# Two empty half periods removed from a pipelined attention, and its PSUM banks split three for scores, two for row maxima

## The chip, the core and the metric

The kernel runs on one core of one Trainium2 chip. The time is device microseconds of that core, for one launch that does the whole layer. It keeps five engines in step by semaphores: PE (TensorE, matrix products), ACT (ScalarE), DVE (VectorE), POOL (GpSimd) and SP, which here only issues DMAs. PSUM, where PE writes its products, has eight banks of 512 float32 columns for each of the 128 partitions.

## The reference

A decoder layer with post-layernorm on `x` (8 sequences of 512 tokens, width 256), in float32:

```python
x = _layernorm(x + _L0_attn_ref(x, Wqkv, Wout))            # 16 heads of 16, rotary q and k, softmax
x = _layernorm(x + _L0_xattn_ref(x, ctx, ctx, w_q, ...))   # 16 heads of 16, biases, softmax
x = _layernorm(x + _L0_ffn_ref(x, gate_w, we_gate, ...))   # 8 experts, top 2, plus shared experts
```

Each of the 16 attention instances (self and cross, for 8 sequences) computes `softmax(q k^T / 4) v` for 16 heads over 512 keys. The change touches the two attentions alone.

## The kernel before, in words

**Instances and halves.** An attention instance is (SELF, b) or (CROSS, b) for sequence b. The program walks through *periods* k, each with a FIRST half, whose instance is (SELF, k), and a SECOND half, whose instance is (CROSS, k-1). A half has 16 *steps*; a step does one block of 128 keys for four heads. The halves that exist run in this order: self 0, self 1, cross 0, self 2, cross 1, ..., self 7, cross 6, cross 7. Between self 0 and self 1 lies the SECOND half of period 0, for which there is no instance (it would be cross -1), and between cross 6 and cross 7 the FIRST half of period 8 (it would be self 8). These are the two empty half periods. They run all their steps, but only with the side tasks of their table and the maxima that run ahead. Periods 2 to 6 are a hardware loop (`Fori`).

**One step on PE** (function `half` of the PE block): for j = 0..3 a score product `ps_sc` (L725, 50 rows x 512 columns, keys on the partitions) and a product `ps_max` (L711, 48 rows x 512 columns, queries on the partitions). Before j = 2 come the head outputs `ps_out` (L742, eight rows of the profile for four heads) of the step before, which need all four exponentials of that step. After j = 1 stands a small transpose of the negated maxima (`nm0`, `nm1`, L697) in one step of four, and after j = 3 the side job of the step, if it has one.

**The two chains beside it.** ACT takes the exponential of each score bank (L477, `prob<-ps_sc`). The maximum that it needs is already inside the score product, as two extra rows of q ("mrows"), because the maxima run 7 steps (`LEAD`) ahead: DVE reduces each `ps_max` bank to one column (L519, `nm<-ps_max`), PE transposes them, ACT and DVE split them into a high and a low part, and SP writes them into row 48 and 49 of `qk`.

**The banks.** Of the eight banks two are for side jobs (`ps_job`), one for head outputs, and five for these products: `NSC, NMX = 2, 3`. Score product n goes to bank n % NSC and waits until the exponential n - NSC is done; maximum product n goes to bank n % NMX and waits until reduction n - NMX is done. PE works its queue strictly in order, so whatever it waits for, all behind it waits too.

**Side tasks.** The tables `TASKS` say at which step which projection, transpose or normalization of a neighbouring sequence is done: `q, k, v, cq, ck, cv` are projections (L629, six products of 512 columns or twelve of 256), `ot` four head transposes (L682), `nt, xt` transposes (L665), `w` the output projection, `ln` the layernorm, `x, c` the split of an input. A side job on PE stands at the end of its step; what ACT and DVE do with its result stands at the *start* of their next step, ahead of that step's exponentials and maxima. On DVE that is for `q, k` the pair L535, L536, for `cq, ck` L503 behind ACT's L388, for `ot` L561, L563, for `nt, xt` L501 or L503 behind ACT's L386 or L388, for `w` L581, L585, L588, for `ln` L597.

**SP.** Projected q and k of an instance are written to HBM (`hbm_self`, `hbm_cross`) and read back in another layout by twelve DMAs for each group of four heads (`stack`), which write `qk`.

Behind the attentions, from about 1150 us, comes the phase of the experts, which the change doesn't touch.

## Time and profile before

| | |
|---|---|
| three runs | 1589.96, 1599.72, 1615.62 us; median 1599.72 |
| the profiled execution | 1609.8 us, its span 1608.1 us, mean granted clock 0.915 |
| busy, of the span | PE 89%, DVE 69%, ACT 56%, weight loads 53%, POOL 27% |
| self 0 starts its scores | 61.1 us |
| self 1 starts its scores | 173.5 us |
| cross 0 starts its scores | 230.8 us |
| cross 6, cross 7 start their scores | 996.5 us, 1094.5 us |

Times of one execution are read from the span's start. In a row of the timeline stand the start, the length, the engine, the line, the operation, output<-input, and in brackets how long the engine had been idle and for whom. Lengths of matrix products are modelled ends and overlap: two products of the row-tiled pair `ps_sc`, `ps_max` run at the same time on different rows of the array. PEclk is the clock that PE was granted: 1.0 is 2.4 GHz, 0.5 is 1.2 GHz.

### The profile page before, as it was taken

The page shows a single profiled execution, that of the slowest core. Times are in us where ns is not written, and L with a number is a line of the kernel's source. Part 1 is how long each engine was busy: PE and PEld are TensorE (multiplying, and loading weights), DVE is VectorE, ACT ScalarE, POOL GpSimd, SP SyncE. Part 2 cuts the span into 40 slices and gives each one's busy share as a digit, 9 for nine tenths or more (in the row PEclk, how much of TensorE's full clock was granted, in tenths as well). Part 3 has the DMA queues.
Part 4 walks back from the last instruction along what each step waited for, and adds up shares of the span by engine and source line. Part 5 has one row for each costly group of instructions (what it writes and reads, how often), then busy time and mean ns, then how long its engine had stood idle before and what let it go on. Part 6 is the DMA issues. An engine that isn't in the chain of part 4 may idle for free. (4 is left out here: it accounts for less than half of the span.)

```text
span 1608.1 us, 27690 instructions
## 1 busy us (share of the span) xinstructions
PE 1434.6 (89%) x8424; PEld 857.3 (53%) x8424; DVE 1113.8 (69%) x2282; ACT 907.7 (56%) x1702; POOL 439.8 (27%) x411
## 2 busy tenths in 40 slices
PE   2987999999999999999999999979768898999994
PEld 2424434435444444454444443343357788999974
DVE  3725788879788889889879877648146654555566
ACT  3361576756666666666766765725425444656544
POOL 4004022014013104104104201100005443666654
PEclk8676899989999999999999997987669889999997
DMA  3313343333333333234234233031035425677662
GB/s 125 115 57 111 110 127 106 122 116 113 109 115 128 103 119 116 76 136 128 78 135 135 87 116 120 2 112 35 1 113 183 147 103 126 133 151 159 136 183 89
DMA packets 108089, 179.85 MB, mean 112 GB/s; under 512 B 20288, under 2 KB 65984, under 8 KB 103872
## 3 DMA queue, kind: packets, MB, share of 16 engines
q1 hardware_dynamic: 93376, 159.11, 30.9%
q0 software_dynamic: 14592, 19.41, 6.7%
q8 instruction: 42, 0.69, 0.2%
q14 instruction: 79, 0.65, 0.1%
HBM read 98.09 MB, written 79.30 MB: 110 GB/s over the span
## 5 line engine op out<-in xcount | busy, mean ns | idle before, releaser
L477 ACT ACTIVATE prob<-ps_sc 128x512 f32<-128x512 f32 x1024 | 557.6, 597 | 272.4 <-PE ps_sc L725 267.8
L519 DVE TENSOR_REDUCE nm<-ps_max 128x1 f32<-128x512 f32 x1024 | 640.7, 681 | 94.3 <-PE ps_max L711 94.3
L711 PE MATMUL ps_max<-qk 48*128 48x512 f32 x1024 | 451.9, 509 | 33.7 <-DVE nm L519 23.0
L725 PE MATMUL ps_sc<-qk 50*128 50x512 f32 x1024 | 415.6, 477 | 41.0 <-ACT prob L477 40.7
L725 PEld LDWEIGHTS ps_sc<-qk 50*128 50x128 f32 x1024 | 170.0, 192 | 370.0 <-ACT prob L477 306.9
L742 PE MATMUL ps_out<-prob,va 128*32 128x512 f32 x2048 | 288.0, 636 | 1.3 <-ACT prob L477 1.2
L711 PEld LDWEIGHTS ps_max<-qk 48*128 48x128 f32 x1024 | 182.6, 198 | 93.1 <-DVE nm L519 73.9
L1475 PE MATMUL ps_gu<-x2f,we 128*128 128x256 f32 (+1 forms) x1344 | 223.8, 321 | 4.5 <-ACT sg L1140 2.4
L1475 PEld LDWEIGHTS ps_gu<-x2f,we 128*128 128x128 f32 x1344 | 190.5, 192 | 22.2 <-DVE h L1366 3.0
L356 POOL TENSOR_TENSOR rstd<-mv,eps 128x2 f32<-128x2 f32 x32 | 6.5, 203 | 595.8 <-DVE mv L588 595.8
L1475 PE MATMUL ps_dn<-we,hf 128*128 128x256 f32 x864 | 122.8, 298 | 10.6 <-DVE totals L1449 10.6
L1475 PEld LDWEIGHTS ps_dn<-we,hf 128*128 128x128 f32 x864 | 116.8, 205 | 12.1 <-DVE hf L1370 11.6
L629 PE MATMUL ps_job<-xf,w 128*128 128x512 f32 x288 | 86.0, 438 | 22.5 <-POOL xf L331 16.7
L629 PE MATMUL ps_job<-w,cf 128*128 128x256 f32 x576 | 86.5, 303 | 5.1 <-DVE cf L503 1.7
L1064 POOL DMA_INDIRECT slots_x<-x2in,scat x64 | 66.1, 1033 | 87.6 <-DVE r L1306 27.7
L629 PEld LDWEIGHTS ps_job<-w,cf 128*128 128x128 f32 x576 | 76.7, 203 | 17.3 <-issue 11.1
L742 PEld LDWEIGHTS ps_out<-prob,va 128*32 128x32 f32 x2048 | 41.1, 110 | 69.9 <-issue 59.4
L629 PEld LDWEIGHTS ps_job<-xf,w 128*128 128x128 f32 x288 | 55.0, 205 | 43.1 <-issue 25.6
L1078 POOL DMA_INDIRECT sums<-ys,dest x40 | 62.2, 1555 | 49.4 <-DVE dest L1407 26.1
L1078 POOL DMA_INDIRECT x<-ys,dest x40 | 62.1, 1553 | 31.2 <-ACT ys L1205 18.9
L340 POOL TENSOR_TENSOR res<-res,trig 128x512 f32<-128x512 f32 x32 | 41.0, 1280 | 107.3 <-DVE res L536 107.3
L1222 ACT ACTIVATE hf<-h 128x512 fp32r<-128x512 f32 x40 | 25.3, 632 | 63.4 <-DVE h L1424 57.0
(145 smaller groups left out, 1472.9 us busy)
## 6 DMA issues: line engine op xcount, KB each, us to landing
qk<-hbm_self SPq DMA_DIRECT2D x384, 64.0 KB, 2.3
qk<-hbm_cross SPq DMA_DIRECT2D x384, 64.0 KB, 2.3
hbm_self<-stage SPq DMA_DIRECT2D x16, 1024.0 KB, 3.9
hbm_cross<-stage SPq DMA_DIRECT2D x16, 1024.0 KB, 4.8
slots_x<-zeros SPq DMA_DIRECT2D x8, 1360.0 KB, 5.9
xs<-slots_x SPq DMA_DIRECT2D x40, 272.0 KB
weraw<-w_moe SPq DMA_DIRECT2D x11, 768.0 KB
x2in<-x SPq DMA_DIRECT2D x16, 512.0 KB, 4.0
```

The source lines that it names most:

```text
L340: nc.gpsimd.tensor_tensor(rot[:, c, :], rot[:, c, :], trig[:, 1, :], ALU.mult) \
L356: nc.gpsimd.tensor_tensor(rstd[:, at, :], mv[:, at, 1:2], eps[:, at, :], ALU.add) \
L477: nc.scalar.activation(prob[:, s % 2, j, :], ps_sc[:, (HG * s + j) % NSC, :], ACT.Exp, scale=HD ** -0.5).then_inc(exp_done[a], 1)
L519: nc.vector.tensor_reduce(nm[:, g % 2, r:r + 1], ps_max[:, n % NMX, :], axis=AX.X, op=ALU.max, negate=True).then_inc(max_done[a], 1)
L629: ins = nc.tensor.matmul(out, l(a), r(b), start=(n == 0 and k == 0), stop=(n == len(pairs) - 1 and k == len(parts) - 1))
L711: nc.tensor.matmul(ps_max[:, n % NMX, :], qk[rows, 0, pair, P * c:P * c + P], qk[rows, 1, pair, :], start=True, stop=True).then_inc(smax_d ...
L725: nc.tensor.matmul(ps_sc[:, n % NSC, :], qk[rows, 1, h // 2, P * c:P * c + P], qk[rows, 0, h // 2, :], start=True, stop=True).then_inc(st_ ...
L742: ins = nc.tensor.matmul(ps_out[32 * j:32 * j + 32, :], va[:, a, c, HG * g + j, :], prob[:, s % 2, j, :], start=(c == 0), stop=(c == TT - ...
L1064: nc.gpsimd.indirect_dma_start(rows_x, bass.IndirectOffsetOnAxis(ap=scat[:, q, c, t:t + 1], axis=0), xin[:, q, t, :], None, bounds_check=P ...
L1078: nc.gpsimd.indirect_dma_start(x2 if j // NCH else sums, bass.IndirectOffsetOnAxis(ap=dest[:, c, t:t + 1], axis=0), ys[:, c, t, :], None, ...
L1222: nc.scalar.activation(hf[:, p, HI, :, 0:CH], h[:, p, :].rearrange("p (c t) -> p c t", c=IC), ACT.Copy).then_inc(hhi_done, 1)
L1475: ins = nc.tensor.matmul(o, l(a), r(b), start=(n == 0 and k == 0), stop=(n == len(pairs) - 1 and k == len(parts) - 1))
```

## The change

It has two parts. First, the tables are no longer only FIRST and SECOND: a `Half` object carries its own table, instance, neighbours and SP duties. The order becomes lead, own, own0 (self 0), *close* (self 1), *gap*, second(1) (cross 0), the same loop over periods 2 to 6, first(7) (self 7), *close* (cross 6), *gap*, last (cross 7), post. In *close* the side tasks of its own half and of the empty half stand together, up to two jobs a step; it makes its own maxima to step 8, none in steps 9 to 13, and those of the next instance from step 14. The *gap* has 5 steps without scores: 20 maxima of the next instance, `cv`, `nm1` and `cv`. Second, `NSC, NMX = 3, 2`.

```diff
-NSC, NMX = 2, 3
+NSC, NMX = 3, 2
...
+OWN0 = {
+    0: [("qf", 0, 1), ("k", 0, 1)], 1: [("nm0", 1, 0)], 2: [("kf", 0, 1), ("q", 1, 1)], 3: [("k", 1, 1)], 4: [("qf", 1, 1)],
+    5: [("nm0", 2, 0), ("kf", 1, 1)], 9: [("nm0", 3, 0)], 13: [("nm0", 0, 1)],
+}
+GAP, START = 5, 14
...
+    return {
+        0: [("v", 0, b + 1), ("v", 1, b + 1)], 1: [(rows, 1, i), ("ot0", 0, b), ("ot0", 1, b)], 2: [("ot0", 2, b), ("ot0", 3, b)],
+        3: [("nt0", 0, b), ("nt0", 1, b)], 4: [("w0", 0, b)], 5: [(rows, 2, i), ("w0", 1, b), ("c", 0, b)], 6: [("ln0", 0, b)],
+        7: [("xt", 0, b), ("xt", 1, b)], 8: [("ck", 0, b)], 9: [(rows, 3, i), ("cq", 0, b)], 10: [("cq", 1, b)],
+        11: [("ck", 1, b)], 12: [("x", 0, b + 2)], 13: [("x1b", 0, b)] if b + 1 < B else [], 15: [("q", 0, b + 2)],
+    }
...
+    return {1: [("cv", 0, b)], 2: [("nm1", 0, b), ("cv", 1, b)]}
...
+LAST = {
+    1: [("nm1", 1, 1), ("ot1", 0, 0)], 2: [("ot1", 1, 0)], 3: [("ot1", 2, 0)], 4: [("ot1", 3, 0)], 5: [("nm1", 2, 1)],
+    7: [("nt1", 0, 0)], 8: [("nt1", 1, 0)], 9: [("nm1", 3, 1), ("w1", 0, 0)], 10: [("w1", 1, 0)], 12: [("ln1", 0, 0)],
+    13: [("x1b", 0, 1)],
+}
...
+    own.loads = {8: [("x", 1)]}
+    own.table = {**own.table, 11: [("x", 0, 1)], 15: [("q", 0, 1)]}
...
+    own1 = Half("close", close_behind("nm0", 1, 0), [], s1, c0, s0, None, s0, start=START,
+                loads={2: [("c", 0)], 11: [("x", 2), ("xin", 1)]}, cross={10: (0, 0), 13: (0, 1)},
+                stacks={0: (s1, s0, 3), 12: (c0, s1, 0), 13: (c0, s1, 1)}, clear=1)
+    gap = Half("gap", gap_of(0), own1.table[15], None, c0, s1, s0, s1, steps=GAP, start=START - STEPS,
+               stacks={0: (c0, s1, 2)})
...
+    late = Half("close", table, [], c6, c7, s7, (CROSS, B - 3), s7, start=START,
+                loads={2: [("c", B - 1)]}, cross={10: (B - 1, 0), 13: (B - 1, 1)},
+                stacks={0: (c6, s7, 3), 12: (c7, c6, 0), 13: (c7, c6, 1)})
...
-            for k in (-1, 0, 1):
-                half(FIRST, k)
-                half(SECOND, k)
+            for h in before_loop():
+                half(h)
             with eng.Fori(2, B - 1) as k:
-                half(FIRST, k)
-                half(SECOND, k)
-            for k in (B - 1, B, B + 1):
-                half(FIRST, k)
-                half(SECOND, k)
...
+        def maxima_of(h, s):
+
+            if s >= h.start:
+                inst, first = h.nxt, TT * (s - h.start)
+            else:
+                inst, first = h.cur, TT * (s + LEAD)
+            return [(inst, n) for n in range(first, first + TT)] if inst and first < NMAX else []
```

In the loop the order of the instructions is the same on every engine; only the bank and the count in the waits of `ps_sc` and `ps_max` change. Outside it the order moves at these places.

DVE, before: part of the first empty half period, the side tasks of sequence 0 (`nt0`, `w0`, `ln0`, `xt`) with the maxima of self 1, and no exponentials beside them on ACT.

```order
L501 TENSOR_TENSOR cf<-ps_job,cf 128x512 x2
L581 TENSOR_TENSOR res<-ps_job,xin 128x512
L585 BN_STATS st<-res 128x6 x2
L588 BN_AGGR mv<-st 128x2 x2
L519 TENSOR_REDUCE nm<-ps_max 128x1 x4
L581 TENSOR_TENSOR res<-ps_job,xin 128x512
L585 BN_STATS st<-res 128x6 x2
L588 BN_AGGR mv<-st 128x2 x2
L519 TENSOR_REDUCE nm<-ps_max 128x1 x8
L597 TENSOR_SCALAR x<-res,mv,rstd 128x256 x4
```

DVE, now: the same tasks stand in the close half of self 1 (line numbers are those of the changed kernel), each between the four maxima of a step.

```order
L600 TENSOR_TENSOR cf<-ps_job,cf 128x512 x2
L618 TENSOR_REDUCE nm<-ps_max 128x1 x4
L680 TENSOR_TENSOR res<-ps_job,xin 128x512
L684 BN_STATS st<-res 128x6 x2
L687 BN_AGGR mv<-st 128x2 x2
L618 TENSOR_REDUCE nm<-ps_max 128x1 x2
L600 TENSOR_TENSOR mst<-ps_job,mst 16x128
L618 TENSOR_REDUCE nm<-ps_max 128x1 x2
L680 TENSOR_TENSOR res<-ps_job,xin 128x512
L684 BN_STATS st<-res 128x6 x2
L687 BN_AGGR mv<-st 128x2 x2
L618 TENSOR_REDUCE nm<-ps_max 128x1 x4
```

So the tasks that had a half of their own now share their steps with self 1's scores, exponentials and maxima.

PE, now: from the last score product of self 1 to the first of cross 0. This is the whole gap: 20 maximum products, two jobs `cv`, one `nm1`, and at its start the job `q` of sequence 2 and the last head outputs of self 1.

```order
L824 MATMUL ps_sc<-qk 128x512
L810 MATMUL ps_max<-qk 128x512
L727 MATMUL ps_job<-xf,w 128x512 x6
L810 MATMUL ps_max<-qk 128x512 x2
L841 MATMUL ps_out<-prob,va 32x512 x4
L810 MATMUL ps_max<-qk 128x512 x6
L727 MATMUL ps_job<-w,cf 128x256 x12
L810 MATMUL ps_max<-qk 128x512 x2
L796 MATMUL ps_job<-ident,nm 16x128
L810 MATMUL ps_max<-qk 128x512 x2
L727 MATMUL ps_job<-w,cf 128x256 x12
L810 MATMUL ps_max<-qk 128x512 x8
```

Before, PE had in the corresponding place the end of self 0 and then all the jobs of the empty half, of which this is the beginning.

```order
L725 MATMUL ps_sc<-qk 128x512 x2
L629 MATMUL ps_job<-xf,w 128x512 x6
L742 MATMUL ps_out<-prob,va 32x512 x4
L629 MATMUL ps_job<-xf,w 128x512 x6
L682 MATMUL ps_job<-ident,ot 128x128 x8
L629 MATMUL ps_job<-xf,w 128x512 x6
L682 MATMUL ps_job<-ident,ot 128x128 x4
L629 MATMUL ps_job<-xf,w 128x512 x6
```

The projections of sequence 1 seen here moved ahead, into self 0 (`q` of the first half into the step before it), and the transposes behind, into self 1.

## Rows read from the trace of the kernel before

**Rows 1.** Windows, by stage: stretch, us, busy us (count) by engine, PEclk, DMA share, GB/s.
```profile
41.60:61.10 19.50, 18.74 (x41) 10.06 (x42) 15.98 (x28) 0.86 (x2) 0.00 (x0) 0.50 0.46 121
61.10:116.90 55.80, 48.85 (x225) 15.46 (x224) 24.35 (x41) 36.60 (x70) 2.35 (x1) 0.81 0.22 73
116.90:173.50 56.60, 43.32 (x149) 27.24 (x148) 32.26 (x67) 8.35 (x15) 19.27 (x17) 0.62 0.31 93
173.50:230.80 57.30, 52.62 (x303) 21.69 (x302) 43.60 (x72) 40.86 (x78) 5.12 (x5) 0.99 0.41 131
230.80:996.50 765.70, 733.69 (x4317) 352.29 (x4316) 644.96 (x1212) 510.18 (x983) 157.08 (x155) 0.98 0.35 113
996.50:1051.10 54.60, 51.23 (x297) 21.03 (x297) 33.00 (x66) 39.47 (x76) 4.35 (x5) 0.96 0.09 26
1051.10:1094.50 43.40, 32.94 (x130) 20.68 (x129) 27.40 (x56) 6.08 (x10) 4.53 (x8) 0.74 0.37 113
1094.50:1150.00 55.50, 47.97 (x224) 14.96 (x222) 24.45 (x41) 35.50 (x68) 0.00 (x0) 0.81 0.06 18
```

**Rows 2.** Windows, one period of the loop: cross 3 and self 5; columns PE, PEld, DVE, ACT, POOL.
```profile
615.60:677.00 61.40, 59.93 (x365) 29.58 (x364) 54.84 (x106) 42.84 (x83) 19.55 (x17) 1.00 0.30 96
677.00:742.10 65.10, 60.65 (x357) 28.96 (x356) 52.88 (x96) 42.27 (x81) 7.08 (x9) 1.00 0.41 133
```

**Rows 3.** Timeline of PE, one step of self 1 without a side job.
```profile
212.78 0.50 PE L725 MATMUL ps_sc<-qk 50*128 50x512 f32 x1
212.79 0.50 PE L711 MATMUL ps_max<-qk 48*128 48x512 f32 x1
213.97 0.50 PE L725 MATMUL ps_sc<-qk 50*128 50x512 f32 x1 [0.45 <-ACT prob L477]
214.46 0.49 PE L725 MATMUL ps_sc<-qk 50*128 50x512 f32 x1
214.88 1.06 PE L742 MATMUL ps_out<-prob,va 128*32 128x512 f32 x8
215.88 0.50 PE L725 MATMUL ps_sc<-qk 50*128 50x512 f32 x1
```

**Rows 4.** Timeline of DVE and of ACT, the same step.
```profile
213.36 2.48 DVE L519 TENSOR_REDUCE nm<-ps_max 128x1 f32<-128x512 f32 x4 [0.62 <-PE ps_max L711]
...
213.32 2.27 ACT L477 ACTIVATE prob<-ps_sc 128x512 f32<-128x512 f32 x4 [0.83 <-PE ps_sc L725]
```

**Rows 5.** Timeline of PE, then of DVE, a step of cross 3 with a side job.
```profile
617.73 0.50 PE L711 MATMUL ps_max<-qk 48*128 48x512 f32 x1
618.16 1.66 PE L629 MATMUL ps_job<-xf,w 128*128 128x512 f32 x6
...
617.00 2.48 DVE L519 TENSOR_REDUCE nm<-ps_max 128x1 f32<-128x512 f32 x4
619.96 0.69 DVE L535 TENSOR_TENSOR cosq<-ps_job,trig 128x512 f32<-128x512 f32 x1 [0.49 <-PE ps_job L629]
621.22 1.27 DVE L519 TENSOR_REDUCE nm<-ps_max 128x1 f32<-128x512 f32 x2
```

**Rows 6.** Waits of the whole run: engine line <- releaser, us in total, times, longest.
```profile
PE ps_sc L725 <- ACT prob L477: 40.7, 86, 1.3
PE ps_max L711 <- DVE nm L519: 23.0, 43, 1.6
```

**Rows 7.** The page's DMA issues (KB, us to landing), and SP's timeline within one stack.
```profile
qk<-hbm_cross SPq DMA_DIRECT2D x384, 64.0 KB, 2.3
hbm_cross<-stage SPq DMA_DIRECT2D x16, 1024.0 KB, 4.8
...
216.69 5.56 SPq L254 DMA_DIRECT2D qk<-hbm_cross  x10
```

**Rows 8.** Windows, a stretch of the loop at the lower clock, and PE's timeline at it.
```profile
348.50:358.80 10.30, 10.04 (x34) 3.96 (x35) 5.60 (x9) 3.82 (x8) 0.00 (x0) 0.50 0.20 65
...
116.47 2.93 PE L629 MATMUL ps_job<-xf,w 128*128 128x512 f32 x6
```

More of the change, by code:

```diff
@@ L3 @@
 from contextlib import ExitStack
+from dataclasses import dataclass, field
 import numpy as np
@@ L68, in exists, with shifted @@
     return not isinstance(b, int) or 0 <= b < B
+def shifted(table, k):
+    return {s: [(kind, n, k + off) for kind, n, off in table[s] if exists(k + off)] for s in table}
+@dataclass
+class Half:
+    name: str
+    table: dict
+    former: list
+    cur: tuple = None
+    nxt: tuple = None
+    prv: tuple = None
+    older: tuple = None
+    tail: tuple = None
+    steps: int = STEPS
+    start: int = STEPS - LEAD
+    k: object = None
+    loads: dict = field(default_factory=dict)
+    own: dict = field(default_factory=dict)
+    cross: dict = field(default_factory=dict)
+    stacks: dict = field(default_factory=dict)
+    result: dict = field(default_factory=dict)
+    clear: object = None
@@ new lines, in behind_loop @@
+def behind_loop():
+    s7, c6, c7 = (SELF, B - 1), (CROSS, B - 2), (CROSS, B - 1)
+    table = {s: [t for t in row if exists(t[2])] for s, row in close_behind("nm1", B - 2, B - 1).items()}
+    late = Half("close", table, [], c6, c7, s7, (CROSS, B - 3), s7, start=START,
+                loads={2: [("c", B - 1)]}, cross={10: (B - 1, 0), 13: (B - 1, 1)},
+                stacks={0: (c6, s7, 3), 12: (c7, c6, 0), 13: (c7, c6, 1)})
+    gap = Half("gap", gap_of(B - 1), [], None, c7, c6, s7, c6, steps=GAP, start=START - STEPS, stacks={0: (c7, c6, 2)})
+    last = Half("last", shifted(LAST, B - 2), [], c7, None, c6, s7, None, stacks={0: (c7, c6, 3)}, result={14: B - 2})
+    post = Half("post", shifted(TASKS[FIRST], B + 1), [], None, None, c7, c6, c7, result={14: B - 1})
+    return [first(B - 1), late, gap, last, post]
@@ L71, in upto @@
+SPECIAL = [(t, i) for i, t in enumerate(
+    t for h in before_loop()[2:5] + behind_loop()[1:4] for s in sorted(h.table) for t in h.table[s]
+    if t[0] in PER and t[0] not in ("x", "c"))]
+SPECIAL = {t: i % 2 for t, i in SPECIAL}
 def upto(kind, b, n):
@@ L195, in bank, with behind @@
-        def bank(kind, n):
-            return ps_job[:, [t[:2] for t in ORDER].index((kind, n)) % 2, :]
-        def maxima_of(s, cur, nxt):
-            inst, first = (cur, TT * (s + LEAD)) if s + LEAD < STEPS else (nxt, TT * (s + LEAD - STEPS))
-            return [(inst, n) for n in range(first, first + TT)] if inst else []
+                half(first(k))
+                half(second(k))
+            for h in behind_loop():
+                half(h)
+        def behind(h, s):
+            return h.table.get(s - 1, []) if s else h.former
@@ L284, in half @@
-                for s in range(STEPS):
-                    if h == FIRST and s in (1, 6) and exists(k - 1):
-                        m = s // 6
-                        sp.wait_ge(lo_done["cq"], upto("cq", k - 1, m))
-                        sp.wait_ge(lo_done["ck"], upto("ck", k - 1, m))
+                for s in range(h.steps):
+                    if s in h.cross and exists(h.cross[s][0]):
+                        b, m = h.cross[s]
+                        sp.wait_ge(lo_done["cq"], upto("cq", b, m))
+                        sp.wait_ge(lo_done["ck"], upto("ck", b, m))
@@ L331, in split_lo, with half @@
                 nc.gpsimd.tensor_tensor(out, value, high.bitcast(F32), ALU.subtract).then_inc(lo_done[kind], 1)
-            def half(h, k):
-                for s in range(STEPS):
-                    for kind, n, b in tasks(h, s, k):
+            def half(h):
+                for s in range(h.steps):
+                    for kind, n, b in h.table.get(s, []):
                         if kind in ("q", "k"):
@@ L450, in rows_hi, with half @@
                     mrow_wait(cur or prv, 2)
-                split_hi(kind, b, n, mst[:, n % 2, HI, :], bank(kind, n)[0:HG * TT, 0:P])
-            def half(h, k):
-                cur, nxt, prv = instances(h, k)
-                if h == FIRST and isinstance(k, int) and k == 0:
+                split_hi(kind, b, n, mst[:, n % 2, HI, :], bank(kind, n, b)[0:HG * TT, 0:P])
+            def half(h):
+                if h.name == "own0":
                     act.wait_ge(w_ready, 5)
-                older = instances(prv[0], prv[1] + prv[0])[2] if prv else None
-                for s in range(STEPS):
-                    for kind, n, b in former(h, s, k):
+                for s in range(h.steps):
+                    for kind, n, b in behind(h, s):
                         if kind not in ("nm0", "nm1"):
@@ L608, in half @@
                         if j == NM_AT + 1:
-                            for kind, n, b in tasks(h, s, k):
+                            for kind, n, b in h.table.get(s, []):
                                 if kind in ("nm0", "nm1"):
```

245 lines of the change are left out of this document (129 added, 116 removed).

## The prediction

> **What bounds the kernel now.** I read the windows by stage first. From 230.8 to 996.5 us run twelve halves, cross 0 to self 7, in 765.7 us, almost half of the span, at clock 0.98 [rows 1]: whatever the banks do is multiplied there. The empty half periods take 56.6 and 43.4 us; ACT is busy for 8.35 and 6.08 us in them, and the clock is 0.62 and 0.74 [rows 1]. What they hold is worth at most 100 us, and much of it must be done somewhere else.
>
> Then one period of the loop: 61.4 + 65.1 = 126.5 us with DVE busy 54.8 + 52.9 = 107.7, ACT 42.8 + 42.3 = 85.1 [rows 2]. PE reads 120.6, but its lengths are modelled, so I look at what its products wait for. The table of waits gives PE 40.7 us behind exponentials and only 23.0 behind reductions [rows 6]. That speaks for the third score bank, but it counts only time in which no older product was still shown as running. The timelines show more.
>
> In a step without a side job, the products of j = 2 come first in the rows, then those of j = 0 and 1 of the next step. Score product 2 starts at 212.78, its exponential at 213.32, and product 0 of the next step at 213.97, after an idle 0.45; products 1 follow at 214.46, head outputs at 214.88, product 2 again at 215.88 [rows 3, 4]. The step is 3.10 us long, and its chain is 0.54 + 0.65 + 0.49 + 0.42 + 1.00: the score banks set it. In a step with a side job another chain does. DVE's first maximum starts at 617.00; four take 2.48, so with 0.68 for one they start 0.60 apart [rows 5]. The first ends at 617.68, and maximum product 3 starts at 617.73, 0.05 behind it: it waits for n - 3. The job starts 0.43 later (618.16) and is 1.66 long, DVE idles 0.49 for it and starts its task at 619.96, and the next maximum at 621.22 [rows 5]. Product 3 of the next step can start at 621.22 + 0.68 + 0.05 = 621.95: a loop of 4.22 us, through PE's job, DVE's task and the *first* maximum behind it.
>
> **Two maxima banks.** In the step without a job, product 1 of the next step must now wait for the reduction of product 3. Product 2 at 212.79, reductions from 213.36 [rows 3, 4]: the second ends at 213.36 + 0.60 + 0.68 = 214.64, product 1 starts at 214.69, head outputs 0.42 later, product 2 another 1.00 later: 216.11. The step becomes 3.33, 0.23 longer. The third score bank would by itself have let the head outputs start at 213.32 + 0.49 + 0.60 + 0.05 = 214.46 and the step end at 2.68; that gain of 0.42 is lost behind the maximum product, which is in PE's queue ahead of the head outputs.
>
> In the step with a job, product 3 waits for the second maximum and not the first: 0.60 later. The job, DVE's task (it was idle for it) and the next first maximum move by the same 0.60, so each such step pays again: 4.82 for 4.22. Which steps these are, the tables say: all where DVE has a task that depends on the job of the step before: cq, ck twice each, nt1 and w1 twice each in FIRST; q, k, nt0, w0, xt twice each in SECOND: 18 of 32. One of them, the first xt, I take out, since ACT's split of `c` stands in front of its exponentials. 17 x 0.60 = 10.2. The other fifteen: v and cv are followed by no task on DVE and are PE's own length, single steps without a job between others pay little, since their wait is partly paid by the neighbour's; only ln, with four tasks on DVE, costs another 0.6. I add 0.8 for all. That is 11.0 a period, and 6 periods x 11.0 = **66 us** for the twelve halves. Upper bound: all 32 steps by 0.60, 115 us. Lower bound: below zero, because the 40.7 us behind exponentials may go and the maxima be hidden; I put it at -30. I take 66, near the middle, because the step of [rows 5] is what most steps look like.
>
> The trace shows one and the same gap of 0.45 before a score product in the steps without jobs [rows 3]. The Trainium skill, Perfetto Trace Analysis, section Optimization Strategy, says that a gap that repeats on the engine that should be full can mean too few buffers in PSUM. By that rule alone the third score bank would bring back much of the 40.7 us, and the sum would be as in the first rival. It names the right bank for one chain, and doesn't say what the bank taken away was doing.
>
> **The empty halves.** By stage, against [rows 1]:
> - *41.6 to 61.1* (28 maxima at clock 0.5, 19.5 us). With two banks a reduction waits for its product's way: at this clock I take 0.16 more for each, 4.5 us, and the job q of sequence 1 now stands there, up to 2.93 [rows 8], partly hidden: +6 (0 to 8).
> - *Self 0*, 55.8: its last step's projection leaves, three with DVE tasks come in (4.8 each), and the other thirteen steps now all have maxima: 14.5 + 13 x 3.33 + four small transposes of 0.2 = 58.5, +2.7 (0 to 6).
> - *First empty half*, 56.6, goes; the gap of 5 steps comes. 20 maxima at 0.65 to 0.8 are 13 to 16, two jobs cv (1.7 to 2.9) are half hidden: 17 (13 to 22). -39.6.
> - *Self 1*, 57.3, becomes the close half. The nearest rows are the loop's halves, 61.4 and 65.1 [rows 2], which by the sum above become 67 and 70. The close half has a few more side jobs than these, two in a step in places, where DVE does both tasks before it turns to the maxima; but it has no maxima in steps 9 to 13. I take 68; bounds are 61 (a loop half as it was) and 76 (70 and two more job steps' worth of waits). SP's way from the projection to `qk` is 4.8 to HBM, twelve issues at 0.56, 2.3 to land [rows 7], 14 us, against steps 10 to 13, which have two or three jobs and come to about the same: I add 1.5 for a late stack (0 to 5). 69.5, +12.2.
> - *Cross 6*, 54.6, becomes the other close half, without v, x and q, three jobs of 1.66 less [rows 5], some of it covered: 64 + 2 = 66, +11.4.
> - *Second empty half*, 43.4, for a gap of 17: -26.4.
> - *Cross 7*, 55.5: ot1, nt1, w1 join it. Its last steps have no maxima and gain from three score banks (3.1 to 2.7), the others pay: 57, +1.5.
>
> These make 6 + 2.7 - 39.6 + 12.2 + 11.4 - 26.4 + 1.5 = **-32 us**. Bounds of the unknown parts: -45 to -12.
>
> **The clock.** Two stretches of some 10 us in the loop are at 0.5; one is shown [rows 8]. It holds 34 of PE's products in 10.3 us; a step without job has 16, so it takes 4.8 there for 3.1, and one stretch costs about 3 us. The two lie at the end of self 2 and of self 3, where DVE does ln1 and PE waits longest. With 0.6 more waiting in each step I expect it in three more periods: **+9** (0 to 30).
>
> Sum: -32 + 66 + 9 = +43, 1609.8 + 43 = 1653 for the profiled execution, a ratio of 1.027. That execution is 10 us above the median of the three runs; by the ratio on 1599.7 I forecast **1642 us**.
>
> **Rivals.**
> - *The score banks matter, the maxima banks don't.* For it: the waits, 40.7 against 23.0 [rows 6], and ACT's idle 0.83 in each step [rows 4]. Against: product 3 starts just 0.05 behind a reduction [rows 5]. If DVE's queue had room, the halves would keep 765.7 less some 15 to 20, the other stages lose 5 us less, and the clock nothing: 1600 - 32 - 20 = 1548. Chance 0.12.
> - *The two parts cancel.* If in half of the seventeen steps the third score bank or ACT's slack catches the 0.60 (as I assume for one xt), the loop pays 30: 1600 - 32 + 30 + 3 = 1601. For it: several ACT tasks stand in front of exponentials. Chance 0.15.
> - *The clock falls again and again.* PE now stops twice in every step, for DVE. The trace shows 0.98 for the loop [rows 1] and falls only where PE waits longest. If each half had one more stretch at 1.2 GHz of 10 us, 3 to 6 us each in twelve halves with longer jobs (2.93 for 1.66 [rows 5, 8]): 1642 + 50 = 1690 to 1700. Chance 0.12. The Trainium skill, TensorE: Matmul & The Clock Gate, section "A second HAM failure mode: psum-queue depth-cycling", tells of a kernel whose cycling through PSUM banks leaves micro-idles and makes the clock swing. By that rule this case is the likeliest; the trace before, with such waits in every step and the clock at 0.98, bears it out only little.
> - *My forecast*, the chain through the second maximum: 0.61, its own range 1615 to 1675.
>
> **Range and chances.** 1592 to 1695 us: it takes in the whole forecast, most of the cancelling case and most of the clock's. A change of 2% (1568, 1632) is about what this kernel's runs, 1590 to 1616, can tell from none. Faster by more: the first rival, 0.12. Within: the second and the lower fifth of the forecast, 0.29. Slower: 0.59.
>
> **What would show it.** In the loop, a step without job of 3.3 and a job step q or k of 4.8; PE's `ps_max` waits for `nm` up several times, `ps_sc` waits for `prob` nearly gone; period 137 us for 126.5; DVE busy unchanged at 108 in a longer period. The close halves 66 to 70, the gaps 15 to 19. I would be wrong if product 3 starts before the second reduction has ended, which would mean that the banks don't bind as I read them; if the period stays at 127; or if the close halves are far over 70, because a stack or a side task comes late.

## The result and the profile after

The changed kernel took 1675.57 us in the median of four runs (1674.49 to 1684.47), the kernel before, beside it on the same chip, 1598.95 (1589.96 to 1615.62). The ratio is 1.0511, with a 95% interval of 1.0449 to 1.0573: **slower**, by 5% where 2.7% were forecast. (The ratio is that of the means without the execution of 1615.62 us, a slow one, over 1.5% above the fastest of its kernel.) The profiled execution took 1675.1 us (its span 1673.4, mean granted clock 0.901) against 1608.1 for the span before. All stage times below are of these two spans, 65.3 us apart.

The windows by stage, as in [rows 1]: prologue to self 0, self 0, close half of self 1, gap, the twelve halves of the loop, close half of cross 6, gap. A stage begins where its scores start, a gap where the first of its 20 maximum products starts (205.75 and 1137.06). What is called the loop here is the stretch of twelve halves from cross 0 to self 7, of which the ten in the middle are the hardware loop.

```profile
41.60:68.80 27.20, 23.89 (x47) 11.83 (x47) 18.26 (x29) 1.81 (x3) 2.35 (x1) 0.50 0.58 128
68.80:128.60 59.80, 53.20 (x271) 21.50 (x270) 46.80 (x80) 38.57 (x75) 15.34 (x12) 0.97 0.37 114
128.60:205.70 77.10, 70.25 (x349) 33.04 (x349) 42.06 (x78) 45.08 (x83) 9.22 (x10) 0.82 0.38 112
205.70:224.20 18.50, 15.37 (x54) 8.40 (x54) 13.26 (x23) 2.06 (x4) 2.53 (x2) 0.78 0.08 24
224.20:1067.60 843.40, 815.00 (x4307) 387.03 (x4305) 654.61 (x1211) 519.39 (x982) 154.06 (x153) 0.95 0.33 102
...
1067.60:1137.10 69.50, 65.70 (x320) 28.78 (x320) 41.64 (x78) 42.70 (x80) 4.12 (x5) 0.84 0.26 78
1137.10:1156.90 19.80, 16.89 (x54) 8.76 (x54) 12.95 (x21) 2.32 (x5) 0.00 (x0) 0.67 0.21 50
```

The largest number is the loop's: 843.4 us for 765.7 [rows 1], +77.7, with DVE's busy time up by only 10 in it. The empty halves did go (18.5 and 19.8 us stand where 56.6 and 43.4 were), but the halves beside them grew.

One period of the loop, cross 3 and self 5, as in [rows 2], and the first job step of that cross half on PE and DVE, as in [rows 5].

```profile
643.80:710.60 66.80, 65.61 (x365) 31.86 (x364) 55.80 (x106) 43.82 (x83) 19.52 (x17) 1.00 0.29 88
710.60:786.60 76.00, 71.59 (x357) 33.33 (x356) 53.99 (x96) 42.96 (x81) 7.05 (x9) 0.89 0.38 115
```

```profile
645.90 0.50 PE L810 MATMUL ps_max<-qk 48*128 48x512 f32 x1
...
646.50 0.49 PE L810 MATMUL ps_max<-qk 48*128 48x512 f32 x1
646.92 1.66 PE L727 MATMUL ps_job<-xf,w 128*128 128x512 f32 x6
...
651.30 0.50 PE L810 MATMUL ps_max<-qk 48*128 48x512 f32 x1
```

```profile
645.17 2.55 DVE L618 TENSOR_REDUCE nm<-ps_max 128x1 f32<-128x512 f32 x4
```

The first reduction ends at 645.17 + 0.68 = 645.85, and maximum product 2 starts at 645.90; the second ends 0.60 later, at 646.45, product 3 starts at 646.50, and the job behind it at 646.92. Before, product 3 stood 0.05 behind the *first* reduction [rows 5]. From product 3 to product 3 it is 651.30 - 646.50 = 4.80 us; 4.82 was forecast.

That this holds step after step can be read from the starts of the steps. In cross 3, at full clock in both traces, the 16 steps differ from before by 0.59, 0.60, 0.02, 0.59, 0.60, -0.24, 0.01, 0.59, 0.52, 0.60, 0.61, -0.59, 1.20, -0.25, 0.23 and 0.37 us: 5.4 in all, and eight of them by 0.52 to 0.61. The first fourteen steps of self 2 ran at full clock too, before and now, and grew by 5.0:

```profile
291.95:347.44 55.49, 52.83 (x319) 25.90 (x319) 46.28 (x85) 37.90 (x73) 7.08 (x9) 1.00 0.45 145
```

```profile
293.31:353.81 60.50, 57.49 (x320) 27.59 (x319) 47.66 (x87) 38.22 (x73) 7.05 (x9) 1.00 0.44 133
```

A step without a job, on PE and on DVE, as in [rows 3, 4], here from self 0.

```profile
96.26 0.49 PE L824 MATMUL ps_sc<-qk 50*128 50x512 f32 x1
...
98.17 0.49 PE L810 MATMUL ps_max<-qk 48*128 48x512 f32 x1
98.59 1.07 PE L841 MATMUL ps_out<-prob,va 128*32 128x512 f32 x8
99.59 0.50 PE L824 MATMUL ps_sc<-qk 50*128 50x512 f32 x1
```

```profile
96.82 2.57 DVE L618 TENSOR_REDUCE nm<-ps_max 128x1 f32<-128x512 f32 x4 [0.76 <-PE ps_max L810]
```

The step is 99.59 - 96.26 = 3.33 us, as forecast (3.10 before). Product 1 of the next step, at 98.17, stands behind the second reduction (96.82 + 0.60 + 0.68 = 98.10), and the head outputs stand behind it.

The table of waits, as in [rows 6].

```profile
PEld ps_sc L824 <- ACT prob L576: 189.5, 244, 2.5
PEld ps_max L810 <- DVE nm L618: 180.2, 404, 2.1
```

Against those of before:

```profile
PEld ps_sc L725 <- ACT prob L477: 306.9, 444, 2.2
...
PEld ps_max L711 <- DVE nm L519: 73.9, 152, 2.1
```

Waits for a maxima bank went from 73.9 to 180.2 us and from 152 to 404 times; those for a score bank fell from 306.9 to 189.5. In this profile most of a wait for a bank is on the row of the weight load (180.2 us for `ps_max`), and the matmul's own row [rows 6] shows what is left: 23.0 us for `ps_max` are up to 43.5, 40.7 for `ps_sc` down to 5.7. So "`ps_sc` waits nearly gone" holds for the matmul's row alone, and "`ps_max` several times" is 2.4 times on one row and 1.9 on the other.

### The profile page after: what moved, and what is told of

It is laid out like the page before. It is cut to its first block and busy times, and to the rows that moved or that the text cites. A ratio compares the mean times of both kernels' runs of the same rounds, so it can differ in the third digit from the quotient of the medians.

```text
span 1673.4 us, 27725 instructions
## 1 busy us (share of the span) xinstructions
PE 1526.5 (91%) x8424; PEld 901.0 (54%) x8424; DVE 1132.1 (68%) x2282; ACT 917.9 (55%) x1702; POOL 438.7 (26%) x411
## 5 line engine op out<-in xcount | busy, mean ns | idle before, releaser
L618 DVE TENSOR_REDUCE nm<-ps_max 128x1 f32<-128x512 f32 x1024 | 657.5, 684 | 162.4 <-PE ps_max L810 161.8
L576 ACT ACTIVATE prob<-ps_sc 128x512 f32<-128x512 f32 x1024 | 566.5, 597 | 362.9 <-PE ps_sc L824 357.4
L810 PE MATMUL ps_max<-qk 48*128 48x512 f32 x1024 | 473.4, 519 | 60.3 <-DVE nm L618 43.5
L824 PEld LDWEIGHTS ps_sc<-qk 50*128 50x128 f32 x1024 | 179.5, 200 | 291.3 <-ACT prob L576 189.5
L841 PE MATMUL ps_out<-prob,va 128*32 128x512 f32 x2048 | 299.4, 659 | 2.9 <-ACT ot L503 1.7
L810 PEld LDWEIGHTS ps_max<-qk 48*128 48x128 f32 x1024 | 187.2, 201 | 209.6 <-DVE nm L618 180.2
L1573 PE MATMUL ps_dn<-we,hf 128*128 128x256 f32 x864 | 128.5, 307 | 13.3 <-DVE totals L1547 10.5
L1573 PEld LDWEIGHTS ps_dn<-we,hf 128*128 128x128 f32 x864 | 122.2, 214 | 15.1 <-DVE hf L1468 14.5
L727 PE MATMUL ps_job<-xf,w 128*128 128x512 f32 x288 | 88.4, 448 | 20.1 <-POOL xf L433 16.5
L602 DVE SCALAR_TENSOR_TENSOR stage<-ps_job,bcol,stage 128x512 fp32r<-128x512 f32 x32 | 24.0, 751 | 60.2 <-ACT stage L490 60.2
```

Source lines behind the costliest of these rows:

```text
L576: nc.scalar.activation(prob[:, s % 2, j, :], ps_sc[:, (HG * s + j) % NSC, :], ACT.Exp, scale=HD ** -0.5).then_inc(exp_done[a], 1)
L602: ins = nc.vector.scalar_tensor_tensor(out=out, in0=value, scalar=bias, in1=high.bitcast(F32), op0=ALU.add, op1=ALU.subtract)
L618: nc.vector.tensor_reduce(nm[:, g % 2, r:r + 1], ps_max[:, n % NMX, :], axis=AX.X, op=ALU.max, negate=True).then_inc(max_done[a], 1)
L727: ins = nc.tensor.matmul(out, l(a), r(b), start=(n == 0 and k == 0), stop=(n == len(pairs) - 1 and k == len(parts) - 1))
L810: nc.tensor.matmul(ps_max[:, n % NMX, :], qk[rows, 0, pair, P * c:P * c + P], qk[rows, 1, pair, :], start=True, stop=True).then_inc(smax_d ...
L824: nc.tensor.matmul(ps_sc[:, n % NSC, :], qk[rows, 1, h // 2, P * c:P * c + P], qk[rows, 0, h // 2, :], start=True, stop=True).then_inc(st_ ...
```

## The experiments

The theory at the start: product 3 waits for the second reduction, and with it the job, DVE's task and the next reductions; that is the loop's loss. The rivals: it comes with the new halves, from the score banks, or from the clock. The two parts of the change, run apart, are called p1 and p2. Times of stages below are of one profiled execution each, and not all on the same chip; ratios are to the kernel before on the same chip.

**The new halves alone** (p1), with the old banks:

```diff
-NSC, NMX = 3, 2
+NSC, NMX = 2, 3
```

> The new halves with the old banks (two for scores, three for maxima). Theory (the banks cost the time, the halves save some): the twelve halves of the loop stretch are back at 766 us, 61.4 for a cross and 65 for a self half, and the total is the time before less about 30: 1568 (1555 to 1580). Rival (the close halves are where the time goes, through a late stack and a late load of x): the total stays above 1600.

Measured: 1569.26 us (1563.78 to 1570.21), ratio 0.9791 [0.9748, 0.9834]. Its first close half with gap, and the loop:

```profile
118.70:208.60 89.90, 80.92 (x402) 38.09 (x403) 54.02 (x101) 46.70 (x87) 11.74 (x12) 0.86 0.34 99
208.60:969.20 760.60, 727.80 (x4309) 351.24 (x4307) 644.47 (x1211) 509.82 (x982) 154.41 (x153) 0.98 0.37 114
```

The loop is as before (760.6 for 765.7). Taking out the empty halves is by itself a gain of about 2%, and the loop's loss has nothing to do with it.

**The banks alone** (p2), with the old halves:

```diff
-NSC, NMX = 2, 3
+NSC, NMX = 3, 2
```

> The old halves with the new banks (three for scores, two for maxima). Theory: every loop half is as long as in the changed kernel, cross 66.8, twelve halves 843, and the total is 1599 plus 77 plus 5 to 10 for the other halves: 1684 (1675 to 1695), more than the changed kernel. Rival (the halves are to blame): 1600 to 1620.

Measured: 1705.41 us (1695.71 to 1713.16), ratio 1.0645 [1.0587, 1.0703]. The stretch from self 0's scores to self 1's, and the loop:

```profile
66.00:182.90 116.90, 95.30 (x371) 45.47 (x369) 57.96 (x108) 44.33 (x84) 21.64 (x18) 0.73 0.27 80
245.60:1088.30 842.70, 811.81 (x4317) 385.72 (x4316) 655.99 (x1212) 520.01 (x983) 157.00 (x155) 0.96 0.33 103
```

The loop's loss is here: 842.7 (843.4 with both parts), and cross 3 takes 66.8, the same as with both. The total is 21 over what I expected, and that lies outside the loop: 97.1 of span, 77.0 in the loop, 14.8 ahead of it, 5.3 behind. The two parts nearly add up: -39.7 + 97.1 = 57.4 of span, 65.3 with both.

**Neither bank: two and two**, old halves. It tells what each third bank is worth.

```diff
-NSC, NMX = 2, 3
+NSC, NMX = 2, 2
```

> The old halves with two score banks and two maxima banks, one bank of PSUM unused. Theory (the chain through the second maximum sets almost every step, so that a third score bank buys nothing while maxima have two): cross halves of 67 to 68 us, product 3 still 0.60 behind the end of the first reduction, total within 10 us above the kernel with three and two: 1685 to 1695. Rival (the third score bank does pay in the steps without a job and where ACT is late, and hides part of the loss): 0.3 to 0.4 us in each of some 15 steps a period and more, 1705 to 1725.

Measured: 1737.41 us (1730.93 to 1745.77), ratio 1.0851 [1.0793, 1.0909]. Self 0 with the empty half, the loop, cross 3, and everything from cross 7 on:

```profile
65.30:191.50 126.20, 103.42 (x371) 47.99 (x369) 57.79 (x108) 45.34 (x84) 21.62 (x18) 0.64 0.25 75
254.20:1101.20 847.00, 810.64 (x4315) 388.62 (x4314) 657.03 (x1212) 521.35 (x983) 157.03 (x155) 0.95 0.33 102
680.30:747.40 67.10, 65.55 (x366) 32.19 (x365) 55.81 (x106) 43.90 (x83) 19.53 (x17) 1.00 0.28 86
1209.00:1739.00 530.00, 461.86 (x2944) 393.04 (x2942) 277.79 (x726) 252.85 (x459) 227.87 (x197) 0.84 0.45 116
```

In the loop the third score bank buys 847.0 - 842.7 = 4.3 us, 0.3 of a cross half; the third maxima bank, against the kernel before, buys 847.0 - 765.7 = 81.3 us, 67.1 - 61.4 = 5.7 of cross 3. So it is as the theory says there, and the rival of the score banks falls. The total came out over 40 us above my figure, beyond the rival's too (1705 to 1725), and most of that lies where the clock is lower: the first stretch has 0.64 for p2's 0.73 and is 9.3 longer, the last 0.84 for 0.89 and is 530.0 for 514.3. What moves the clock there I did not isolate.

**Head outputs one place earlier**, in the changed kernel: if PE's wait for a maxima bank could stand behind the head outputs, they would hide it.

```diff
-PV_AT = 2
+PV_AT = 1
```

> The changed kernel with the head outputs one place earlier in PE's order, before the products of j = 1 and not of j = 2. Theory: in a step without a side job the head outputs no longer stand behind the maximum product that waits for the last reduction, so these steps go from 3.33 to about 3.15 us; the steps with a job keep their 4.8, since product 3 still waits for the second maximum; total 5 to 12 us less than the changed kernel, 1664 to 1671. Rival (the order on PE is what makes DVE's waits, in all steps): 30 us or more less, below 1645.

Measured: 1737.84 us (1724.50 to 1769.03), ratio 1.0823 [1.0754, 1.0892], 62 more than the changed kernel (50 by the two ratios) where I expected less. PE in self 0, then PE and DVE at the start of cross 3:

```profile
98.70 0.50 PE L810 MATMUL ps_max<-qk 48*128 48x512 f32 x1
99.13 1.06 PE L841 MATMUL ps_out<-prob,va 128*32 128x512 f32 x8
```

```profile
666.27 0.50 PE L810 MATMUL ps_max<-qk 48*128 48x512 f32 x1
...
667.59 0.50 PE L810 MATMUL ps_max<-qk 48*128 48x512 f32 x1 [0.15 <-DVE nm L618]
```

```profile
666.84 1.97 DVE L618 TENSOR_REDUCE nm<-ps_max 128x1 f32<-128x512 f32 x3 [0.19 <-PE ps_max L810]
```

The steps without a job stayed at 3.33 (96.79 to 100.12) and didn't fall to 3.15: the head outputs at 99.13 now stand behind product 0, at 98.70, and that one waits for a second reduction too (97.36 + 0.60 + 0.68 = 98.64). In the step with a job, maximum product 1 now comes behind the head outputs, at 666.27. The second reduction starts late for it (666.84), ends at 667.52, and product 3, which waits for it, starts at 667.59, 2.97 behind product 0 (664.62) where the changed kernel has 646.50 - 643.81 = 2.69. I had counted what the move takes from the score chain and forgotten that the maximum product feeds the very reduction that binds. In this step a late *second* reduction is paid in full, 0.28. It is a small part of the loss: cross 3 takes 70.5 us for 66.8, and it grows most in its steps 2, 5, 6 and 11, by 0.5 to 1.1 each, whose chain was not read.

**The loads of x earlier**, on p1 (new halves, old banks). In the changed kernel's first close half, steps 13 and 14 take 6.95 and 7.73 us. SP, then ACT and PE, there:

```profile
176.59 0.63 SPq L399 DMA_DIRECT2D slots_x<-zeros  x1
...
181.00 1.32 SPq L365 DMA_DIRECT2D raw<-xT  x1
...
184.37 5.54 SPq L352 DMA_DIRECT2D qk<-hbm_cross  x12
```

```profile
188.21 1.06 ACT L488 ACTIVATE xf<-raw 128x1024 fp32r<-128x1024 f32 x1 [3.22 <-DMA raw<-xT]
...
193.98 0.80 PE L810 MATMUL ps_max<-qk 48*128 48x512 f32 x2 [2.90 <-DMA qk<-hbm_cross]
```

The load of `raw` is issued at 181.00, behind the clearing of the experts' buffers, and ACT stands 3.22 us for it, with its exponentials behind. The load of `xin` and then the stack of `qk` (184.37) follow, and PE's maximum products of step 14 stand 2.90 us for the stack.

```diff
-                loads={2: [("c", 0)], 11: [("x", 2), ("xin", 1)]}, ...
+                loads={2: [("c", 0)], 8: [("x", 2), ("xin", 1)]}, ...
```

> The new halves with the old banks, and in the close half of self 1 the loads of x and xin at step 8 of SP's order instead of 11, so that they no longer stand between the write of cross 0's projections and the reading back of its first stack. Theory (these loads and the stack behind them are what made the first close half longer than forecast): ACT no longer waits 3 us for raw, the stack comes 3 us earlier, the first close half and gap go from 89.9 to about 84, the total from 1569 to 1563 to 1565. Rival (the clock and DVE's tasks make the close half long, not SP): no change, 1567 to 1571.

Measured: 1536.70 us against 1577.03 for the kernel before on that chip, ratio 0.9748 [0.9709, 0.9786], the lowest ratio of the runs that compute the whole. The first close half with its gap, self 7, and the second close half with its gap:

```profile
120.50:204.30 83.80, 78.47 (x404) 37.72 (x404) 53.97 (x101) 46.48 (x87) 11.74 (x12) 0.91 0.35 107
907.70:969.50 61.80, 58.20 (x353) 27.09 (x352) 51.24 (x96) 41.61 (x80) 4.55 (x8) 1.00 0.42 131
969.50:1044.00 74.50, 69.33 (x374) 31.93 (x374) 52.57 (x98) 44.23 (x84) 4.13 (x5) 0.97 0.29 83
```

83.8 for p1's 89.9, 6.1 less, as expected, but only half of it is the wait. Step 13 falls from 6.80 to 3.59, which is the 3 us of the theory. Step 8 gives another 2.2 (6.54 to 4.32): it ran at 1.2 GHz in p1 and at 2.4 here, and nothing in the edit is shown to do that. Step 14 still waits for the stack. The total's difference to p1 is within both intervals.

The second close half, with its gap, shows what the clock alone can do. The edit doesn't touch it and its instructions are those of p1, which took 82.2 us for it (969.2 to 1051.4) at clock 0.83; here, on another chip, it is 74.5 at 0.97. Twelve of its sixteen steps are as long to 0.02 us, and nearly all of the 7.7 lies in steps 7 and 8 and in the last one with the gap, where the clocks differ.

**The clearing later too, and a gap of six steps**, on the kernel just seen:

```diff
-GAP, START = 5, 14
+GAP, START = 6, 15
-    return {1: [("cv", 0, b)], 2: [("nm1", 0, b), ("cv", 1, b)]}
+    return {1: [("cv", 0, b)], 3: [("nm1", 0, b), ("cv", 1, b)]}
...
-                    if s == 10 and h.clear is not None:
+                    if s == (15 if h.name == "close" else 10) and h.clear is not None:
```

> As x_load_early, and the clearing DMAs of self 1 at step 15 instead of 10, and the maxima of the next instance begin at step 15 with a gap of 6 steps instead of 14 and 5 (its small transpose one gap step later). Theory (the late stack still holds PE's maximum product in step 14): the wait for qk is gone in both close halves, and since the sixth gap step costs 2.5 to 3 us the total is within 3 us of x_load_early. Rival (the stack costs more than that in both places, since PE stands with everything behind it): 5 to 10 us less than x_load_early.

Measured: 1550.45 us, ratio 0.9841 [0.9799, 0.9883], 14 us more than the run above, where the theory had at most 3 more and the rival less. The first close half with its gap takes 86.4 us, where the five-step gap has 83.8; the second pair takes 78.4 for 74.5. Step 14 no longer waits (4.01 for 6.56 in the first), but the gap grows by more than that. Part of this is the clock again (0.95 for 0.97 in the second pair), and the two profiled executions are equal, 1541.3 and 1540.7 of span, so that the 14 us between the medians can't be placed. By the medians five steps stay.

**PE filled**, banks 2 and 2: two unused products in each step were to keep PE busy, so that the clock stays up and the waits alone remain.

```diff
-NSC, NMX = 2, 3
+NSC, NMX = 2, 2
...
+        ps_fill = ctx.enter_context(nc.psum_tensor("ps_fill", [P, T], F32))
...
+                        if cur and ahead and j % 2:
+                            nc.tensor.matmul(ps_fill[:, :], w[:, HI, 0, 0:P], w[:, HI, 0, 0:T], start=True, stop=True)
```

> The old halves with two and two banks, and in each step with scores and maxima two more products of 128 rows by 512 columns into the unused bank, ahead of the maximum products of j = 1 and j = 3; their result is used by nothing. Theory (PE's longer waits cost a second time through its clock, most of all in self 0, cross 7 and the self halves): the added products stand where PE waits for DVE anyway, the granted clock of the loop goes from 0.93 to near 1, self halves from 76 to 71 or 72, total 1695 to 1715 against 1737. Rival (the clock is not what the wait costs, and added work only lengthens the steps that have no wait): 1745 to 1765.

Measured: 2020.85 us (1996.01 to 2050.97), ratio 1.2768 [1.2678, 1.2858], clock 0.845 in the profiled execution, the longest of the four. The lengthening hides what the run was to show. PE in a cross half, then the whole of self 1:

```profile
891.16 0.50 PE L726 MATMUL ps_sc<-qk 50*128 50x512 f32 x1
891.16 0.50 PE L712 MATMUL ps_max<-qk 48*128 48x512 f32 x1
891.50 0.40 PE L726 MATMUL ps_sc<-qk 50*128 50x512 f32 x1
891.83 0.49 PE L763 MATMUL ps_fill<-w 128*128 128x512 f32 x1
892.25 0.50 PE L712 MATMUL ps_max<-qk 48*128 48x512 f32 x1
```

```profile
213.70:337.30 123.60, 123.15 (x335) 48.01 (x334) 46.98 (x72) 42.15 (x78) 5.09 (x5) 0.50 0.19 60
```

The pair at 891.16 runs side by side; the next two are split by the filler, which takes 0.42, and PE has no gap left in the rows. What the waits cost without the clock can't be read from it. But one thing on the clock can: in self 1 PE was busy for 123.15 of 123.60 us and was granted 1.2 GHz all the time (0.97 in the same half with banks 2 and 2 and no filler). The ends of its products are modelled, but DVE waited 64.8 us for it there: the low clock stood with hardly any idle time of PE.

**The loads of x earlier in the changed kernel**, the same edit with banks 3 and 2:

> The changed kernel, with the loads of x and xin in the close half periods issued at step 8 and not at step 11. Theory (the close halves lost time because the loads of x stood behind the projection's clearing in SP's queue, so that the next stack came late too): step 13 of the first close half falls from 6.95 to about 4, the first close half with its gap from 95.6 to 89 or 90, the whole 5 to 7 us less than the changed kernel, about 1669, a ratio to the kernel before of 1.047. Rival (the stack itself bounds these steps, the load is hidden behind it): close half and gap stay at 95 to 96 and the time at 1675.

Measured: 1666.75 us (1657.05 to 1683.84), ratio 1.0403 [1.0337, 1.0468]. The first close half with its gap takes 90.1 us. Self 7:

```profile
993.20:1060.20 67.00, 63.33 (x351) 29.57 (x350) 52.13 (x96) 42.28 (x80) 4.54 (x8) 1.00 0.39 120
```

90.1 for 95.6, as expected: step 13 gives 3.3 of it (6.95 to 3.62); step 14 is as long as before, 7.75, and waits for the stack; the rest is in step 7 and in the last step with the gap, at other clocks. The total is 9 below the changed kernel, the intervals overlap. This self 7 ran wholly at full clock, as did the one with the old banks above, so 67.0 - 61.8 = 5.2 us is what the banks cost this self half without the clock.

**Short reductions with banks 2 and 3, then 3 and 2**, old halves, both with reductions over 256 columns in place of 512, so that the maxima are over half of the keys:

```diff
-                nc.vector.tensor_reduce(nm[:, g % 2, r:r + 1], ps_max[:, n % NMX, :], axis=AX.X, op=ALU.max,
+                nc.vector.tensor_reduce(nm[:, g % 2, r:r + 1], ps_max[:, n % NMX, 0:T // 2], axis=AX.X, op=ALU.max,
```

> The kernel before (two score banks, three maxima banks), with each maximum reduction over 256 of the 512 columns of its product: the maxima are then over half of the keys, which is the part of the computation that it changes. Theory (a reduction's spacing, 0.60 us for 512 columns, is what the second maxima bank costs): here the spacing is about 0.33; the twelve halves of the loop come out 5 to 25 us below 765.7, since only part of the steps are bound by a reduction. It is the base for the next run. Rival (a fixed latency per bank): no statement on this run alone.

> The same short reductions with three score banks and two maxima banks, the old order of the halves. Theory: product 3 waits for the second reduction, which now ends only 0.33 behind the first: each of 17 steps of a period pays 0.3 or less in place of 0.60, so the twelve halves are 20 to 35 us longer than with banks 2 and 3, not 77, and a cross half 2 to 3 us longer, not 5.4. Rival (what the missing bank costs is a fixed latency between engines, or the score banks' doing, and not the reduction): the twelve halves again 70 to 80 us longer, a cross half 5.4.

Measured: 1555.62 us, ratio 0.9710 [0.9635, 0.9786], and 1583.16, ratio 0.9878 [0.9796, 0.9960]. The loop and cross 3 with 2 and 3:

```profile
221.10:948.40 727.30, 703.04 (x4317) 340.63 (x4316) 458.56 (x1212) 507.73 (x983) 157.23 (x155) 1.00 0.40 119
586.10:646.20 60.10, 58.58 (x365) 28.52 (x364) 39.37 (x106) 42.69 (x83) 19.52 (x17) 1.00 0.34 98
```

With 3 and 2, and then its step 4, DVE and PE:

```profile
227.90:980.50 752.60, 734.26 (x4317) 366.75 (x4316) 462.41 (x1212) 511.69 (x983) 157.13 (x155) 0.98 0.38 115
608.50:669.00 60.50, 60.10 (x365) 30.35 (x364) 39.37 (x106) 42.72 (x83) 19.51 (x17) 0.99 0.32 94
```

```profile
626.38 0.74 DVE L519 TENSOR_REDUCE nm<-ps_max 128x1 f32<-128x256 f32 x2
...
626.85 0.82 PE L711 MATMUL ps_max<-qk 48*128 48x512 f32 x2
```

The wait is still there, with the shorter spacing. The first reduction ends at 626.38 + 0.42 = 626.80 and product 2 starts at 626.85; the second ends at 627.12 and product 3 starts some 0.05 behind it. Step 4 takes 3.23 us (624.96 to 628.19) for 2.90 with banks 2 and 3 (601.99 to 604.89), 0.33 more; with the long reductions it took 3.77 for 3.17, 0.60 more. So the price of the missing bank follows the spacing of the reductions, 0.33 for 0.60, and is no fixed latency.

In the sum that isn't plain. In cross 3 the steps that grow do so by 2.5 us together, which is what I gave the whole half (2 to 3), but others shrink by 2.1 (0.60 in step 11, 0.78 in step 13), and the half is 0.4 longer. That these shrink by the third score bank fits the shorter step 11 in the long-reduction kernels with three of them (2.25 for 2.85 with two) but wasn't run apart here. The loop is 25.3 us longer, within the expected 20 to 35 for a reason that I hadn't given: 2 us of it are in the six cross halves, self 7 has 1.4 at full clock, and much of the rest is the clock of the self halves. At 1.2 GHz are some 37 us of this loop and 3 with banks 2 and 3.

The base run missed its bounds: 38 us below 765.7, not 5 to 25. Cross 3 is 1.3 shorter and self 5 3.7 (65.1 to 61.4), more than I had said, and its loop has clock 1.00 for 0.98.

## Why the prediction was right, and where its sizes were off

Taken in the order of its steps, in spans (before to after):

| step | forecast | measured |
|---|---|---|
| prologue maxima | +6 | +7.7 |
| self 0 | +2.7 | +4.0 |
| first empty half to gap | -39.6 | -38.1 |
| self 1 to close half | +12.2 | +19.8 |
| twelve halves, chain and clock | +66, +9 | +77.7 |
| cross 6 to close half | +11.4 | +14.9 |
| second empty half to gap | -26.4 | -23.6 |
| cross 7 and what follows | +1.5 | +2.9 |
| sum | +43 | +65.3 |

**The chain through the second reduction** is right in place and size. The places: 3.33 and 4.80 per step for a forecast of 3.33 and 4.82, product 3 at 0.05 behind the second reduction. The size: cross 3 pays 66.8 - 61.4 = 5.4 and self 7 5.2 at full clock, 10.6 a period for a forecast of 11.0. Self 7 is a lighter half than those of the hardware loop (61.8 for 65 at full clock); of these none ran through at full clock with the new banks, but the first fourteen steps of self 2 pay 5.0. Times six that is about 64 of the 77.7. That it is the bank and not the halves is shown by the two parts run apart; that it is the maxima bank and not the score bank, by two and two; that its price is the spacing of the reductions, by the short ones. All rested on the step that each such wait is paid again in its own step. The growth of cross 3, step by step, shows it, and this half even has the forecast's nine times 0.60: eight steps of 0.52 to 0.61, and steps 11 and 12 with 0.61 together.

**The score bank** was discounted in the forecast and buys 4.3 us in the loop. What it could do alone was right as well: where no maxima stand in the steps, in cross 7, a step takes 2.67 us with three score banks (1226.00 to 1228.67 with the banks alone) for 3.10 before; 2.68 was forecast. The waits had said 40.7 against 23.0 for it [rows 6]. By the rule on gaps in the Trainium skill, Perfetto Trace Analysis, section Optimization Strategy, the sum would have been 1548; the trace disagrees: the repeated gap of 0.45 is before a score product [rows 3], the bank is added, that wait falls from 40.7 to 5.7 us, and the time moves to the wait behind it in the same queue.

**The clock.** Forecast +9 in the loop; measured 77.7 - 64 = about 14, with 0.95 for 0.98 [rows 1]. I had read two stretches at 1.2 GHz in the loop before; the trace has a third, from 980 us to the end of self 7, 37 us in all, and the changed kernel has nine with 92. A step of 3.33 us takes 4.79 at the lower clock, so by an estimate three tenths of the 55 us more, some 17, are lost, which is near the 14. (My own three stretches were 3.7 us each by the working shown, not 3.) They lie in self halves (0.89 in self 5) and at the start of cross 0 (0.94); cross 1 to 5 have 0.99 or 1.00. The rule in the Trainium skill, TensorE: Matmul & The Clock Gate, section "A second HAM failure mode: psum-queue depth-cycling", would have made the swinging clock the likeliest case, at 1690 to 1700. The trace agrees in direction and not in size. That the added waits cause these falls is argued from the runs at equal work (0.98 with 2 and 3, 0.96 with 3 and 2, 0.95 with 2 and 2). It isn't shown: the run meant to hold the clock up didn't, and its self 1 had 1.2 GHz throughout with PE hardly idle.

**The halves around the loop: the terms that were mis-sized.** I put the parts around the loop at -32; they came to -12.4. The 19.6 between them are of two kinds.
- *The banks outside the loop*, 3 to 5 of it. In the forecast they are 4.5 in the prologue, 13 x 0.23 = 3.0 in self 0, about 5 in each close half (67 and 70 for 61.4 and 65.1) and at most 1.5 in cross 7: 17.5 to 19. With the old halves they pay 97.1 - 77.0 = 20.1; with the new ones, changed kernel against p1, 105.0 - 82.8 = 22.2.
- *The new halves themselves*, the other 15 to 16. Without the banks the forecast is -49.5 to -51, and p1 has -39.7 of span, -5.1 in the loop and -34.6 outside. The first close half with its gap is 24.0 shorter than the empty half and self 1 were together, where the forecast without the banks is 32.4; the second pair 15.8, where it is 20.

Two causes in this second kind show in the rows. One is the load of x, issued behind the clearing, for which I had 1.5 under "a late stack". Issued three steps earlier it gives back 3.2 to 3.3 us in step 13, of 7.6 that the first close half was over (77.1 for 69.5). I had followed SP's way from the projection to `qk` and not the three clearing issues and two loads (of `raw` and `xin`) that stand in the same queue, 176.59 to 184.28, nearly 8 us. The other is the clock. I took the close halves from loop halves at full clock [rows 2], and they ran at 0.82 and 0.84; the second pair alone differs by 7.7 us between two executions of the same instructions, at 0.83 and 0.97. What lowers the clock in these stages stays open.

**The signs.** The period of cross 3 and self 5 is 66.8 + 76.0 = 142.8 us for a forecast of 67 + 70 = 137: all of the excess is in self 5, which was at clock 0.89. DVE's busy time in it is 109.8 for 108, the gaps are 18.5 and 19.8 for 15 to 19. Of the close halves, for which 66 to 70 was the mark of being right, the second is inside with 69.5 and the first 7 over; "far over 70, because a stack or a side task comes late" was named as what would make me wrong, and for that one it came.

**The total.** By the medians the change costs 77 us for a forecast of 42: nearly twice, and 1675.57 is inside the range of 1592 to 1695 but just past the forecast's own 1615 to 1675. Of the difference the steps of the table hold 22 (19.6 around the loop, 2.7 in it); the other 11 or 12 come from the base: the profiled execution of before lies 10 us above its median, that of the changed kernel on its own. In the chances, the second rival and a fifth of the forecast make 0.15 + 0.12 = 0.27, not 0.29, and slower 0.61, not 0.59.

## What to carry to other kernels

When two consumers draw on one pool of banks through one in-order queue, ask for each which *instance* of its consumer the next product waits for: a bank less is paid by one consumer's spacing (0.60 us here, 0.33 with the short reductions) in each step whose loop goes through that consumer, nine of sixteen in a cross half; a bank more is worth only the time until the next wait in the queue (4.3 us of 847 here). Read both from the start of the product against the end of the consumer (0.05 behind it), not from the totals of the waits. And when work is moved out of an empty stage, walk every queue that it now shares, the DMA issuing one first: here two loads behind a clearing cost some 3.3 us of one step. With them moved and the old banks the kernel takes 0.9748 [0.9709, 0.9786] of the time before; with the new halves alone it is 0.9791 [0.9748, 0.9834], and the two can't be told apart. And when stage times of two traces are compared, put their granted clocks beside them: one stage of the same instructions took 82.2 us at 0.83 and 74.5 at 0.97.

## What the runs showed of the hardware

- A 48- and a 50-row product on different rows of the array start within 0.01 us of each other and a pair takes 0.33 to 0.34 us; one 128-row product of the same 512 columns between the two makes it 0.33, 0.42, 0.43, one after the other (rows of the filled kernel).
- A reduction over 256 columns has a mean of 0.418 us for 0.681 over 512, on 1024 of each, and its spacing falls from 0.60 to 0.33. Halving the columns brought the whole kernel to 0.971 [0.9635, 0.9786] of its time.
- The stretch from cross 7 on, with 726 DVE and 2944 PE instructions in each of these three, took 513.0 us with banks 2 and 3, 514.3 with 3 and 2, and 530.0 with 2 and 2 at clock 0.84 for 0.89. Steps of cross 7 with maxima take 4.79 us at the lower clock (2 and 2) and 3.33 at the higher (3 and 2).
- PE at 1.2 GHz with hardly any idle time: self 1 of the filled kernel, busy for 123.15 of 123.60 us at clock 0.50.
